# A second edge tile per odd turn, projected from x rows that were gathered in stage 1

## The reference

```
q, k, v = feat @ Wq.T + bq, feat @ Wk.T + bk, feat @ Wv.T + bv     # per node
score = clip(einsum('ehd,ehd->eh', q[edge_dst], k[edge_src]) / sqrt(32), -10, 10)
alpha = exp(score - smax[edge_dst]) / den[edge_dst]                # softmax over a node's edges
wv    = segment_sum(alpha * v[edge_src], edge_dst)
x1    = feat + wv @ Wp.T + bp
out   = layernorm(x + x1 + gelu(layernorm(x1) @ W1.T + b1) @ W2.T + b2)
```

## Time and profile before

| | |
|---|---|
| median of 3 runs | 1100.9 us (1094.48, 1103.52, 1100.9) |
| the profiled execution | 1090.93 us, span 1089.1 us |
| PE busy | 970.3 us, 89% |
| DVE busy | 945.9 us, 87% |
| ACT busy | 669.9 us, 62% |
| POOL busy | 746.9 us, 69% |
| granted TensorE clock, mean | 0.971 of full speed |
| DMA | 312.56 MB, 0.9 of the 16 engines' time in most slices |

### The profile page before, as it was taken

How to read it: one execution, slowest core, us unless ns; L and a number is a source line. 1 busy time by engine, 2 the same in 40 slices (tenths; PEclk the granted TensorE clock), 3 DMA queues, 4 the chain that set the end, 5 groups by cost and what they waited for, 6 DMA issues and landing times.

```text
span 1089.1 us, 25372 instructions
## 1 busy us (share of the span) xinstructions
PE 970.3 (89%) x6188; PEld 641.2 (59%) x6188; DVE 945.9 (87%) x1539; ACT 669.9 (62%) x1936; POOL 746.9 (69%) x800
## 2 busy tenths in 40 slices
PE   7997869989998988988988989889898899889897
PEld 6873336655655655565655555556565555555575
DVE  6965989988998988999889999899889989888953
ACT  3233356667677667766756766766675677677442
POOL 3457777777777777777777777777777777777300
PEclk9998788999999999999999999999999999999999
DMA  9999998999999999999989999999999999999510
GB/s 329 358 343 297 316 289 281 290 304 304 283 309 308 291 295 311 303 294 303 316 277 306 310 292 303 296 322 284 293 324 282 298 314 300 288 314 304 180 37 31
DMA packets 154924, 312.56 MB, mean 287 GB/s; under 512 B 32199, under 2 KB 73125, under 8 KB 154790
## 3 DMA queue, kind: packets, MB, share of 16 engines
q0 software_dynamic: 61536, 200.85, 57.6%
q1 hardware_dynamic: 93254, 110.43, 31.4%
HBM read 269.76 MB, written 41.16 MB: 285 GB/s over the span
## 4 chain that ended last, share of the span: by engine, by line
PE 23%; DVE 23%; issue 22%; DMA 16%; POOL 8%; ACT 5%; SPq 1%; DVEq 1%; ACTq 0%; POOLq 0%
DMA kv<-kv_rows,src_sb 13%; POOL kv L401 8%; DVE score L1640 7%; PE quad L880 6%; DVE kv L1653 4%; PE bank L483 4%; DVE prod L1633 3%; PE bank L503 3%; PE bank L952 2%; DMA agg_in<-agg_rows 2%; PE quad L943 2%; PE quad L483 1%; DVE onehot L1619 1%; PE bank L931 1%; ACT hid L496 1%
## 5 line engine op out<-in xcount | busy, mean ns | idle before, releaser
L401 POOL DMA_INDIRECT kv<-kv_rows,src_sb x750 | 710.7, 948 | 231.8 <-issue 212.2
L1633 DVE TENSOR_TENSOR prod<-kv,quad 128x1024 f32<-128x1024 f32 x196 | 239.2, 1220 | 64.5 <-DMA kv<-kv_rows,src_sb 56.5
L1653 DVE TENSOR_TENSOR kv<-kv,bank 128x1024 f32<-128x1024 f32 x196 | 238.1, 1215 | 1.8 <-ACT kv L1217 1.8
L1640 DVE TENSOR_REDUCE score<-prod 128x32 f32<-128x1024 f32 x196 | 237.7, 1213 | 0.8
L483 PE MATMUL bank<-hT,w_sb 128*128 128x256 f32 x736 | 180.3, 389 | 0.4 <-ACT hid L491 0.4
L503 PE MATMUL bank<-w_sb,hid 128*128 128x256 f32 x736 | 178.3, 392 | 0.0
L943 PE MATMUL quad<-qwin,onehotT 32*128 32x256 f32 x1568 | 101.2, 332 | 74.6 <-DVE prod L1633 72.2
L943 PEld LDWEIGHTS quad<-qwin,onehotT 32*128 32x128 f32 x1568 | 61.0, 186 | 164.4 <-DVE prod L1633 88.9
L503 PEld LDWEIGHTS bank<-w_sb,hid 128*128 128x128 f32 x736 | 140.8, 197 | 23.9 <-issue 5.6
L483 PEld LDWEIGHTS bank<-hT,w_sb 128*128 128x128 f32 x736 | 137.5, 192 | 24.6 <-issue 1.3
L952 PE MATMUL bank<-kv,onehot 128*32 128x264 f32 x1568 | 130.7, 406 | 21.4 <-ACT acc_sb L1231 11.6
(11 more groups left out here) (163 smaller groups left out, 1276.7 us busy)
## 6 DMA issues: line engine op xcount, KB each, us to landing
qwin<-q_rows SPq DMA_DIRECT2D x388, 64.0 KB
dst_rows<-edge_dstT SPq DMA_DIRECT2D x50, 256.0 KB, 5.0
q_rows<-q_next SPq DMA_DIRECT2D x25, 512.0 KB, 4.1
kv_rows<-kv_out SPq DMA_DIRECT2D x24, 512.0 KB, 4.9
kv<-kv_rows,src_sb POOLq DMA_INDIRECT x750
agg_rows<-acc_sb SPq DMA_DIRECT2D x98, 82.5 KB
xT_sb<-xT SPq DMA_DIRECT2D x25, 256.0 KB, 5.2
xq_sb<-xT SPq DMA_DIRECT2D x25, 256.0 KB, 8.8
```

What stands on the lines that cost most here:

```text
L401: return nc.gpsimd.indirect_dma_start(out=rows, out_offset=None, in_=kv_dram, in_offset=bass.IndirectOffsetOnAxis(ap=index, axis=0))
L1633: nc.vector.tensor_tensor(prod[:, slot % 2].rearrange("p (i c) -> p i c", c=C), kv[:, slot, :, 0:C], quad[:, :, 0:C], ALU.mult).then_inc(s ...
L1640: nc.vector.tensor_reduce(score[:, slot % 2], prod[:, slot % 2].rearrange("p (h d) -> p h d", d=HD), AX.X, ALU.add).then_inc(s_score, 1)
L1653: nc.vector.tensor_tensor(kv[:, slot, :, C:2 * C].rearrange("p i (h d) -> p i h d", d=HD), kv[:, slot, :, C:2 * C].rearrange("p i (h d) -> ...
```

## The change

In every odd turn from turn 3 to turn 23 (11 turns) a second tile, the fourth of slot 6, is no longer gathered as k and v. Its x rows are gathered in stage 1 (43 x gathers instead of 32; those beyond the tenth lie in a larger `xg`), and the gates that spread these gathers over stage 1 are moved from 14/9 to 14/13 of a projected half unit for each. In the turn:

- ACT copies the second tile's rows to `second_rows` at the end of its node steps of slot 3.
- PE transposes them in slot 4, behind the output projection, into the other half of bank 7 (`transpose_second`), and projects them behind the sums of slot 4 (`project_second`).
- ACT's `copy_x_columns` of slot 4 now waits for both transposes. The second tile's columns are copied behind the node steps of slot 4 (`copy_second_columns`), so behind the gelu.
- ACT copies the second tile's k and v to `kv[:, 6, 3]` ahead of the node steps of slot 5 (`copy_second_kv`). PE waits for that before it projects the first tile, since both use bank 7.
- DVE waits for it ahead of the products of slot 6.

```diff
+SECOND_SLOT = 6
+    X_SECOND = [(turn, SECOND_SLOT, X_TILE) for turn in range(TURNS) if second_x(turn, turn % 2)]
+    X_ROWS = len(X_TILES) + len(X_SECOND)
...
+def second_x(turn, parity):
+    return parity == 1 and x_turn(turn)
...
-            for k in range(len(X_TILES)):
-                pool.wait_ge(s_mm, min(4 + 14 * k // 9, KV_HALVES))
+            for k in range(X_ROWS):
+                pool.wait_ge(s_mm, min(4 + 14 * k // 13, KV_HALVES))
...
-                    for t in range(gathered(n) - len(x_tiles(turn, i))):
+                    for t in range(gathered(n) - len(x_tiles(turn, i)) - second_tiles(turn, i, parity)):
...
+            def transpose_second(turn, r):
+                pe.wait_ge(s_xrow, x_count(turn, r) + 2 - X_EARLY)
+                transpose_x(None, second_rows, bank7, SB)
+
+            def project_second(turn, r):
+                project_x(x_count(turn, r) + 1, second_columns)
...
                     if i != 5:
-                        node_steps(turn, i)
+                        node_steps(turn, i, r)
+                    if i + 3 == X_SLOT and second_x(turn, parity):
+                        transpose_second(turn, r)
                     if exists(n - 2, BATCHES):
                         sums(n - 2, (i - 2) % SLOTS, 4 * turn + (i - 2) // 2)
+                    if i + 3 == X_SLOT and second_x(turn, parity):
+                        project_second(turn, r)
+                    if i + 2 == X_SLOT and second_x(turn, parity):
+                        pe.wait_ge(s_xkv, x_count(turn, r) + 1)
                     if i == 5:
-                        node_steps(turn, i)
+                        node_steps(turn, i, r)
...
+            def copy_second_rows(turn, r):
+                act.wait_ge(s_xgT, x_count(turn, r))
+                nc.scalar.activation(second_rows[:], xg[:, bass.ds(r + (len(X_TILES) - X_EARLY - 1), 1), :]
+                                     .rearrange("p k n -> p (k n)"), ACT.Copy).then_inc(s_xrow, 1)
+
+            def copy_second_columns(turn, r):
+                act.wait_ge(s_xgT, x_count(turn, r) + 2)
+                nc.scalar.activation(second_columns[:].rearrange("p k n -> p (k n)"), bank7[:, SB:SB + KC * P], ACT.Copy)\
+                    .then_inc(s_xgTc, 1)
+
+            def copy_second_kv(turn, r):
+                act.wait_ge(s_xkvm, x_count(turn, r) + 1)
+                act.wait_ge(s_part, SLOTS * (turn - 1) + SECOND_SLOT + 1)
+                nc.scalar.activation(kv[:, SECOND_SLOT, X_TILE, 0:2 * C], bank7[:], ACT.Copy).then_inc(s_xkv, 1)
+
+            def copy_x_columns(k, transposed=1):
+                act.wait_ge(s_xgT, k + transposed)
...
-                    copy_x_columns(x_index(turn, X_SLOT))
+                    copy_x_columns(x_count(turn, r), 2 if second_x(turn, parity) else 1)
...
-                    node_steps(turn, i)
+                    if i + 2 == X_SLOT and second_x(turn, parity):
+                        copy_second_kv(turn, r)
+                    node_steps(turn, i, r, parity)
+                    if i + 4 == X_SLOT and second_x(turn, parity):
+                        copy_second_rows(turn, r)
+                    if i + 3 == X_SLOT and second_x(turn, parity):
+                        copy_second_columns(turn, r)
...
+                if second_tiles(turn, slot, parity):
+                    dve.wait_ge(s_xkv, x_count(turn, r) + 1)
```

More of the change, by code:

```diff
@@ L51, in configure @@
     global UNITS, ROWS, SUPERBLOCKS, FIRST_ROWS, WINDOWS, CHECKED, Q_UNITS, Q_CHECKED, LAST_TILES
-    global KV_HALVES, LOOPED, LOOP_FROM, X_TURN, X_TILES, X_EARLY
+    global KV_HALVES, LOOPED, LOOP_FROM, X_TURN, X_TILES, X_EARLY, X_SECOND, X_ROWS
     NODES, EDGES = nodes, edges
@@ L101, in x_index, with second_tiles, x_count, kv_done @@
     return max(k for k, (u, b, t) in enumerate(X_TILES) if (u, b) == (turn, i))
-def kv_done(turn, i):
-    if isinstance(turn, int):
-        return sum(16 * (TILES - len(x_tiles(u, i))) for u in range(turn + 1))
-    each = 16 * (TILES - len(x_tiles(turn, i)))
-    return turn * each + (kv_done(LOOP_FROM, i) - LOOP_FROM * each)
+def second_x(turn, parity):
+    return parity == 1 and x_turn(turn)
+def second_tiles(turn, i, parity):
+    return 1 if i == SECOND_SLOT and second_x(turn, parity) else 0
+def x_count(turn, r):
+    return x_index(turn, X_SLOT) + (r - 1 if not isinstance(r, int) or r else 0)
+def kv_done(turn, i, r, parity):
+    if isinstance(turn, int):
+        return sum(16 * (TILES - len(x_tiles(u, i)) - second_tiles(u, i, u % 2)) for u in range(turn + 1))
+    even = 16 * (TILES - len(x_tiles(turn, i)))
+    both = 2 * even - 16 * second_tiles(turn, i, 1)
+    base = kv_done(LOOP_FROM, i, LOOP_FROM // 2, 0) - LOOP_FROM // 2 * both
+    return r * both + (base + parity * (both - even))
 configure(6250, 100000)
@@ L155, in gnn_program @@
         least = sb("least", [1, 4])
-        xg = sb("xg", [P, max(len(X_TILES) - X_EARLY, 1), C])
+        xg = sb("xg", [P, max(X_ROWS - X_EARLY, 1), C])
         xgT = sb("xgT", [P, KC, P])
-        x_src_sb = sb("x_src_sb", [P, len(X_TILES)], i32)
+        second_rows = sb("second_rows", [P, C])
+        second_columns = sb("second_columns", [P, KC, P])
+        x_src_sb = sb("x_src_sb", [P, X_ROWS], i32)
         src_sb = sb("src_sb", [P, 4, HALF], i32)
@@ L656, in load_next_rows, with load_sources @@
                 load_destination_rows(turn + 1, t)
-            def load_sources(turn, parity, t):
+            def load_sources(turn, r, parity, t):
                 for b in range(4):
-                    sp.wait_ge(s_kv[4 * t + b], kv_done(turn, 4 * t + b))
+                    sp.wait_ge(s_kv[4 * t + b], kv_done(turn, 4 * t + b, r, parity))
                     sp.sem_inc(s_gate_sp, 1)
@@ L732, in edges @@
                     if i % 4 == 3 and (not isinstance(turn, int) or 2 * turn + 4 + i // 4 < HALVES):
-                        load_sources(turn, parity, i // 4)
+                        load_sources(turn, r, parity, i // 4)
                     if i == 4 and exists(turn, Q_UNITS - EARLY_Q):
@@ L1063, in last_ffn1, with node_steps @@
                 ffn1_pair(pair, quad[:, bank]).then_inc(f_f1, 1)
-            def node_steps(turn, i):
+            def node_steps(turn, i, r):
                 ends = isinstance(turn, int) and turn == TURNS - 1
@@ L1077, in node_steps @@
                         pe.wait_ge(f_ev, 4 * (turn - 1))
-                    k = x_index(turn, X_SLOT)
-                    pe.wait_ge(s_xrow, k - X_EARLY + 1)
+                    k = x_count(turn, r)
+                    pe.wait_ge(s_xrow, k + (1 - X_EARLY))
                     transpose_x(k, distance)
                 if i + 2 == X_SLOT and x_turn(turn):
-                    project_x(x_index(turn, X_SLOT), xgT)
+                    project_x(x_count(turn, r), xgT)
                 if i == 1 and exists(turn, Q_UNITS - EARLY_Q):
@@ L1356, in last_gelus, with node_steps @@
                                          ACT.Gelu, bias=b1_sb[:, f:f + 1]).then_inc(f_tail, 1)
-            def node_steps(turn, i):
+            def node_steps(turn, i, r, parity):
                 ends = isinstance(turn, int) and turn == TURNS - 1
@@ L1363, in node_steps @@
                 if i + 1 == X_SLOT and x_turn(turn):
-                    copy_x_kv(x_index(turn, X_SLOT), (turn, X_SLOT), X_TILE)
+                    copy_x_kv(x_count(turn, r) + second_tiles(turn, SECOND_SLOT, parity), (turn, X_SLOT), X_TILE)
                 if i == 2 and exists(turn, Q_UNITS - EARLY_Q):
@@ L1624, in onehots, with products @@
                                         ALU.is_equal)
-            def products(n, slot, turn):
-                dve.wait_ge(s_kv[slot], kv_done(turn, slot) - 16 * (TILES - gathered(n)))
+            def products(n, slot, turn, r, parity):
+                dve.wait_ge(s_kv[slot], kv_done(turn, slot, r, parity) - 16 * (TILES - gathered(n)))
                 if x_tiles(turn, slot):
-                    dve.wait_ge(s_xkv, x_index(turn, slot) + 1)
+                    early = isinstance(turn, int) and (turn < X_TURN or slot != X_SLOT)
+                    done = x_index(turn, slot) if early else x_count(turn, r) + second_tiles(turn, SECOND_SLOT, parity)
+                    dve.wait_ge(s_xkv, done + 1)
+                if second_tiles(turn, slot, parity):
+                    dve.wait_ge(s_xkv, x_count(turn, r) + 1)
                 dve.wait_ge(s_qe, n + 1)
@@ L1745, in edges @@
                     if exists(n, BATCHES):
-                        products(n, i, turn)
+                        products(n, i, turn, r, parity)
                     if i % 2 == 0 and exists(4 * turn + i // 2, PAIRS):
@@ L1887 @@
         "x": x,
-        "x_src": src.reshape(EDGE_COLS, P)[order][[(SLOTS * turn + i) * TILES + t for turn, i, t in X_TILES]].T,
+        "x_src": src.reshape(EDGE_COLS, P)[order][[(SLOTS * turn + i) * TILES + t for turn, i, t in X_TILES + X_SECOND]].T,
         "w_qkvT": np.concatenate([a[p + "Wq"], a[p + "Wk"], a[p + "Wv"]], axis=0).T,
```

4 lines of the change are left out of this document (1 added, 3 removed).

## The result

The changed kernel takes **1173.8 us** (median of four runs, 1167.42 to 1179.71), the kernel before beside it 1101.3 us (four runs): a ratio of **1.0675**, 95% interval 1.0616 to 1.0734. It is 72 us slower. The forecast was 1130, so the sign was right and the loss more than twice as large. The profiled execution took 1174.6 us, span 1172.8. Some executions of a kernel take 1.5 to 3.5% longer than its fastest ones, and those are left out of every ratio.

What follows compares the result with a forecast made beforehand. POOL's gathers set 77.5 us a pair, the arithmetic's 74.1 close behind; the change lifts the latter to 79.3, +20 us, plus 9 for the clock: 1090.9 + 29 = 1120 profiled, 1130 us as median, range 1109 to 1144.

Steps and rivals of the forecast that it cites:

- The chain (steps 1 to 6): Odd turn, slots 4 to 7: second columns copied behind the gelu, PE waits 3.4 us, DVE's products of slots 6 and 7 late.
- The arithmetic's limit of 74.1 us a pair: DVE, PE and ACT, never waiting for rows, need 74.1 us per two turns: POOL's 77.5 less 3.4 of DVE's waits.
- 4.20: Odd turn: DVE's products of slot 6 start at 541.78 instead of 537.58 us without its wait for rows.
- 1.04: Odd turn: from DVE's products of slot 6 to those of slot 7 takes 7.92 us instead of 6.88.
- 1.8: Pair of turns: the arithmetic's new limit of 79.3 us is 1.8 above the 77.5 before; eleven pairs, +20 us.
- The clock term of 9 us: PE behind its new wait in odd turns: half speed loses 1.08 us in about three of four turns, +9 us.
- upper bound of 1.7 a turn: Clock loss in an odd turn if the whole 3.4 us half-speed stretch is work: 3.4 / 2 = 1.7 us.
- Step 7: After DVE's products of slot 7: PE has no gap left there, DVE goes on at its own rate; nothing added.
- Rival D: More than the sum: delay lasts beyond slot 7, POOL waits, node loads late, half speed every odd turn; 1151 us, chance 0.13.
- POOL's 13.8 us: One gather of 1.25 us less in each odd turn: 13.8 us gained over eleven if nothing else moved.
- stage 1 at 0: Eleven more x gathers in stage 1 cost 0 us, bounds -2 and +3.

Runs made afterwards that it cites:

- Experiment 2: The changed kernel with ACT's copy of the second columns moved ahead of the gelu: 1.066; with its k and v copy also moved, straight behind the gelu: 1.006.
- filled kernel: The changed kernel with seven idle PE products between the sums of slot 4 and the second projection in odd turns: 1.035, 1134.8 us.
- experiment 4: The kernel before without the fourth gather of slot 6 in odd turns and nothing in its place, that tile using old rows: 0.988 at 1095 us.

## Why the prediction was right in sign and wrong in size

**The chain (steps 1 to 6)** is confirmed, nearly to the tenth. PE's wait was forecast at 3.4 us and is 3.38; with the clock out of the way it is 8.38 us from slot 5 to 6 (forecast 8.37) and 8.04 to slot 7 (7.92). Experiment 2 shows that ACT's order is the cause, and its first half that moving the first alone is not enough. The second alone was not moved in any run. The table load has no pause behind it: the gelu starts at 737.00, after a load from 735.70 of 1.28 us. The drain of which the Trainium skill, "ScalarE: Activation LUTs", section "What ACT_TABLE_LOAD costs", speaks is not there in these rows either.

**The arithmetic's limit of 74.1 us a pair** is the first step that failed. I took DVE's waits for rows, 1.7 us a turn, off the period as if they were all to be had. The filled kernel, where the clock is nearly out of the way, shows in which turns that goes wrong.

In the odd turn my numbers make 38.5 - 1.7 + 4.20 + 1.04 = 42.0 us, and 42.0 is measured. That is luck. Without a wait for rows DVE takes 11.97 us from slot 5 to 7 (experiment 4) and not 13.88 - 2.83 = 11.05. And the filled kernel, at 16.42, is 4.45 above that and not 5.24, because I had counted the +1.04 from 6.88, where 7.89 stands once DVE waits for ACT. The two errors cancel.

In the even turn they do not. My numbers make 39.2 - 1.7 = 37.5 us; 39.5 is measured (39.1 in five of the eight turns, 41.7 and 40.4 in two that hold 6.8 us of half speed each). This is 2.0 us a pair, 22 us in all. The waits for rows are gone there, and others have come up. DVE of the filled kernel in turn 22, slots 3 and 6:

```profile
994.61 0.17 DVE L425 TENSOR_SCALAR den<-agg_in 128x16 f32<-128x16 f32 x1 [1.30 <-DMA agg_in<-agg_rows]
...
1007.03 0.42 DVE L1675 TENSOR_TENSOR onehot<-dloc,bank 128x256 f32<-128x256 f32 x1 [0.29 <-ACT kv L1252]
...
1009.09 0.17 DVE L538 TENSOR_SCALAR root<-mv 128x4 f32<-128x4 f32 x1 [0.50 <-ACT hn L1352]
```

The first is the load of the node sums. DVE waits for it 1.3 us in the mean of the even turns, 0.5 in the kernel before; why it comes later I did not trace. The pair is 81.5 us against 77.7 before, so 3.8 where I had 1.8: some 40 us in place of 20, and the filled kernel's ratio says 39 (31 to 47). The trace of before already held the waits for ACT, in turn 12, where a delay in slot 1 had made up for the wait for rows. DVE there:

```profile
575.25 1.22 DVE L1633 TENSOR_TENSOR prod<-kv,quad 128x1024 f32<-128x1024 f32 x1
...
579.32 1.22 DVE L1633 TENSOR_TENSOR prod<-kv,quad 128x1024 f32<-128x1024 f32 x1
581.05 0.42 DVE L1619 TENSOR_TENSOR onehot<-dloc,bank 128x256 f32<-128x256 f32 x1 [0.51 <-ACT kv L1217]
...
583.10 0.17 DVE L519 TENSOR_SCALAR root<-mv 128x4 f32<-128x4 f32 x1 [0.50 <-ACT hn L1302]
```

Products of slot 6 without a wait, and the same two waits of 0.5 us behind them as in experiment 4. I had read turn 11 alone.

**The clock term of 9 us** is the second: it is 35 (the change less the filled kernel; 34 by the time at half speed). I took one stretch of 3.4 us with 1.08 us lost, in 0.8 of the turns, from the earlier trace rows. That half speed would come, and come on the path, was right. Its length was wrong. In turn 15 it lasts 10.2 us with PE busy throughout, and costs (10.41 - 8.38) + (10.78 - 8.04) = 4.8 us. Over the odd turns 7 to 21 the mean is 3.4. (The row itself gives 1.00 lost and not 1.08, since eight of twelve products that take 2.86 us take 1.91; that is under 1 us of the term.) My upper bound of 1.7 a turn supposed that a stretch ends after 3.4 us, for which one row stood. The Trainium skill, "TensorE: Matmul & The Clock Gate", section "HAM oscillation — how this bites in real kernels", has a loop with a long wait in each step fall to half speed each time; the trace agrees for the odd turns, all eleven, and the price is three times the 12 us that I gave it.

**Step 7**, "I add nothing", holds for the odd turn: outside slots 5 to 7 it takes 25.6 us in the kernel before, in the filled one and in the change. It missed the even turn behind it, as above. In the change POOL waits up to 5.4 us for PE. Rival D had these: POOL waiting, loads for the node part late (here those of the node sums), half speed in every odd turn. It priced them at 1151, with 19 us for the clock and 11 for the rest where 35 and some 20 are measured.

**POOL's 13.8 us** and **stage 1 at 0** were right: 13.6 (10 to 18) and 0.9 measured. The gain that was hoped for is real, it only needs the tile to come from somewhere at no cost.

The sum, measured: 39 us for the filled kernel over the kernel before, in which stage 1's 0.9 is contained, and 35 for the clock make 74; the medians are 72 apart. The 35 is itself a difference of ratios, so the independent check on it is the 34 us by the time at half speed.

## What to carry to other kernels

A wait is worth only what no later wait takes up again: before taking it off a period, look for a turn in which it happens to be missing and see how long that turn is. A new wait of a few us for TensorE is to be priced with the clock behind it, and if the engine stays busy at half speed on the path, the price can be larger than that of the wait; idle products in the wait show in one run how large it is. And a copy that frees a bank is as much on the path as the one that fills it: moving one of two late copies moved the wait and gained nothing, moving both took nine tenths of the loss away.

## What I had not expected of the hardware

- The granted clock stayed at 0.50 for 10.2 us after a wait of 3.38 us, and for 13.7 us where two products of the second projection were left out, with PE busy 3.3 to 3.4 of every 3.4 us, the first 3.4 us of the second case (2.25) aside. Filling the wait with idle products raised the mean clock of the whole execution from 0.943 to 0.975 and made it 39 us shorter (1173.8 and 1134.8, in two sets of runs).
- The same kernel before took 1095 to 1101 us in three measurements and 1381 to 1391 us in three others, on other chips, with a granted clock of 0.85 to 0.89 in the executions profiled there. There the ratios of the change (1.049) and of the filler (1.031) are smaller and half speed is everywhere (355 us in the change). Why these chips are slower stays open.
